# A graph layer whose edge attributes are copied by ScalarE into unused PSUM columns

## The reference

```python
h = jnp.maximum(_layernorm(x, axis=-1), 0.0)          # node_input
w = relu(radial @ W_fc1 / sqrt(10)) * sqrt(2) @ W_fc2 / sqrt(100)   # per edge, 192 wide
w0, w1, w2, w3 = (w[:, :64], w[:, 64:128], w[:, 128:160], w[:, 160:192])
y0 = l0[edge_src]; y1 = l1[edge_src]                  # rows of the linear map of h
e0 = edge_attr[:, :1]; e1 = edge_attr[:, 1:4]
m0 = w0 * y0 * e0
m1 = (w1 * y0)[:, :, None] * e1[:, None, :]
m2 = (w2 * e0)[:, :, None] * y1
m3 = w3 * jnp.einsum('eud,ed->eu', y1, e1) * INV_SQRT3
s0 ... s3 = segment_sum(m0 ... m3, edge_dst)
o0 = (s0 @ W_l2_00 + s3 @ W_l2_10) * a / FAN_L2
o1 = (s1 @ W_l2_01 + s2 @ W_l2_11) * a / FAN_L2
return x + concat(si0 + 0.5 * o0, si1 + 0.5 * o1)
```

## Time and profile before

| | |
|---|---|
| median of 3 runs | 2946.77 us |
| lowest, highest | 2910.21, 2948.76 us |
| the profiled execution | 2931.67 us |
| its span, first to last instruction | 2929.9 us |
| mean granted TensorE clock | 0.749 of full |
| busy: TensorE, VectorE, GpSimd, ScalarE | 2518.0, 1661.1, 1617.6, 340.0 us |
| GpSimd's idle time before its gathers | 1274.2 us |

### The profile page before, as it was taken

One profiled execution on the slowest core, in us unless ns is written; L12 is line 12 of the kernel. 1 busy time (PEld: TensorE's weight loads), 2 busy tenths in 40 slices (PEclk: granted clock), 3 DMA queues, 4 the chain that ended last, 5 costly groups with the idle time before them and its releaser, 6 DMA issues.

```text
span 2929.9 us, 41982 instructions
## 1 busy us (share of the span) xinstructions
PE 2518.0 (86%) x11466; PEld 2003.8 (68%) x11466; DVE 1661.1 (57%) x4639; ACT 340.0 (12%) x636; POOL 1617.6 (55%) x1637
## 2 busy tenths in 40 slices
PE   6889888788989988888888888898888889898888
PEld 6667776667767766666666666676676677676677
DVE  5455656556656556555655555565565556556555
ACT  5000111011101011010101101010110111011111
POOL 4645555555655555545555554555465555555553
PEclk8566778787767687877777777777778777677876
DMA  4212222222222222212222221222122222222221
GB/s 132 58 45 52 54 55 54 51 53 53 56 50 55 53 52 56 52 47 55 50 53 50 54 55 48 52 51 56 46 60 51 50 52 54 50 55 52 51 53 36
DMA packets 160622, 158.30 MB, mean 54 GB/s; under 512 B 87570, under 2 KB 132534, under 8 KB 160602
## 3 DMA queue, kind: packets, MB, share of 16 engines
q0 software_dynamic: 77376, 132.16, 18.3%
q1 hardware_dynamic: 82088, 24.49, 3.7%
q10 hardware_dynamic: 1138, 1.43, 0.1%
HBM read 149.90 MB, written 8.03 MB: 54 GB/s over the span
## 4 chain that ended last, share of the span: by engine, by line
PE 57%; another core or an unknown queue 15%; DVE 13%; issue 10%; DVEq 4%; ACT 1%; DMA 0%; POOL 0%; ACTq 0%; SPq 0%; POOLq 0%
PE ps_w L894 16%; PE ps_s L922 14%; PE ps_s L924 12%; PE ps_h L887 11%; DVE hot L686 3%; DVEq L745 2%; DVE acc L742 2%; DVE dot L661 2%; DVE dots L656 2%; DVE msg L677 1%; DVE hot L680 1%; PE ps_s L910 1%; DVEq L742 1%; PE ps_s L906 1%
## 5 line engine op out<-in xcount | busy, mean ns | idle before, releaser
L381 POOL DMA_INDIRECT y<-table,idx x1612 | 1583.6, 982 | 1274.2 <-DVE msg L677 657.4
L894 PEld LDWEIGHTS ps_w<-w_fc,hr 100*128 100x128 f32 x3224 | 682.8, 241 | 456.9 <-issue 404.2
L894 PE MATMUL ps_w<-w_fc,hr 100*128 100x192 f32 x3224 | 839.2, 417 | 49.2 <-issue 26.8
L922 PE MATMUL ps_s<-hot,msg 128*128 128x128 f32 x3216 | 612.8, 346 | 136.5 <-DVE msg L677 84.9
L922 PEld LDWEIGHTS ps_s<-hot,msg 128*128 128x128 f32 x3216 | 569.3, 255 | 180.6 <-DVE msg L677 111.8
L742 DVE TENSOR_TENSOR acc<-acc,ps_s 64x32 f32 (+1 forms) x1612 | 327.1, 203 | 628.8 <-remote 346.7
L887 PE MATMUL ps_h<-rad,w_fc 10*100 10x512 f32 x806 | 556.8, 775 | 80.0 <-ACT hid_t L492 43.4
L924 PE MATMUL ps_s<-hot,msg 128*128 128x64 f32 x3216 | 531.6, 314 | 88.1 <-issue 87.7
L924 PEld LDWEIGHTS ps_s<-hot,msg 128*128 128x128 f32 x3216 | 521.0, 241 | 94.6 <-issue 94.2
L487 ACT ACTIVATE hr<-ps_h 100x512 f32<-100x512 f32 x403 | 239.3, 597 | 2409.4 <-remote 1012.6
L667 DVE TENSOR_TENSOR msg<-ps_w,y 128x512 f32<-128x512 f32 x404 | 278.9, 690 | 340.9 <-remote 163.9
(11 more groups left out here) (83 smaller groups left out, 537.4 us busy)
## 6 DMA issues: line engine op xcount, KB each, us to landing
y<-table,idx POOLq DMA_INDIRECT x1612
rad<-in_radial SPq DMA_DIRECT2D x202, 40.0 KB
xres<-in_x SPq DMA_DIRECT2D x7, 560.0 KB, 4.7
out<-xres SPq DMA_DIRECT2D x49, 80.0 KB
table<-y SPq DMA_DIRECT2D x6, 560.0 KB, 3.2
idx<-in_src SPq DMA_DIRECT2D x202, 4.0 KB
attr_sb<-in_attr SPq DMA_DIRECT2D x202, 16.0 KB
dst_i<-in_dst ACTq DMA_DIRECT2D x1, 808.0 KB, 7.2
```

What stands on the lines that cost most here:

```text
L381: nc.gpsimd.indirect_dma_start(out=y[:, j, t, :], out_offset=None, in_=table, in_offset=bass.IndirectOffsetOnAxis(ap=idx[:, j // HALF, col ...
L894: ins = nc.tensor.matmul(ps_w[:, s, t, 0:NW], hr[:, s, t * P:(t + 1) * P], w_fc2[:, :], start=True, stop=True)
L922: nc.tensor.matmul(ps_s[:, s, 0:4 * W], msg[:, s, t, 0:P], hot[:, s, t, 1:V, :], start=(t == 0), stop=(t == T - 1))
```

## The change

ScalarE gets an operation more for each group, `move_attr`, right behind the relu. It copies the group's 16 attributes of each partition from `attr_sb` into columns 192 to 195 of the four tiles of `ps_w[:, s]`. It waits for the load of the attributes (which VectorE waited for before) and for the messages of group g - 2, which had that buffer. `edge_dots` and `weigh` read the attributes there. So that the copy, fc2's writes and VectorE's reads of a buffer of `ps_w` never run at the same time, `fc2` waits for the copy (`attr_moved`), and VectorE waits for the copy and for `fc2_done` ahead of `edge_dots`, and not ahead of `scalar_products` as before. In the last group `weigh` also stands behind the wait for fc2.

```diff
@@ functions of the attributes @@
+        def attr_behind(s, a, b, lo=0, hi=T):
+            return ps_w[:, s, lo:hi, NW + a:NW + b]
...
@@ ScalarE @@
+            def move_attr(i, j, first):
+
+                g, s = i * G + j, j % 2
+                if j % HALF == 0:
+                    act.wait_ge(ld_attr[j // HALF], i * 16 + 16)
+                if first:
+                    act.wait_ge(l_done, CHUNKS * NU)
+                else:
+                    act.wait_ge(msg_done, (g - 1) * 4)
+                nc.scalar.activation(attr_behind(s, 0, 4), attr_of(j, 0, 4), ACT.Copy).then_inc(attr_moved, 1)
...
                 def pair(k, first, finish):
                     for j in range(2 * G):
                         relu(k * (2 * G) + j, j % 2, first and j < 2)
+                        move_attr(k * 2 + j // G, j % G, first and j < 2)
...
@@ VectorE @@
-            def edge_dots(j, lo=0, hi=T):
+            def edge_dots(j, factors, lo=0, hi=T):
 
                 nc.vector.tensor_tensor(dots[:, lo:hi, :, :], vectors(j, lo, hi),
-                                        attr_of(j, 1, 4, lo, hi).unsqueeze(3).to_broadcast([P, hi - lo, 3, MUL1]),
+                                        factors.unsqueeze(3).to_broadcast([P, hi - lo, 3, MUL1]),
                                         ALU.mult).then_inc(dots_done, 1)
...
-            def weigh(g, j, s):
+            def weigh(g, s):
                 dve.wait_ge(hot_done, g + 1)
                 nc.vector.tensor_tensor(hot[:, s, :, 1:V, :], hot[:, s, :, 0:1, :].to_broadcast([P, T, 4, W]),
-                                        attr_of(j, 0, 4).unsqueeze(3).to_broadcast([P, T, 4, W]), ALU.mult).then_inc(msg_done, 1)
+                                        attr_behind(s, 0, 4).unsqueeze(3).to_broadcast([P, T, 4, W]), ALU.mult).then_inc(msg_done, 1)
 
             def messages(i, j):
                 g, s = i * G + j, j % 2
-                if j % HALF == 0:
-                    dve.wait_ge(ld_attr[j // HALF], i * 16 + 16)
                 which(g, s)
                 dve.wait_ge(gathered[j], i * (16 * T) + 16 * T)
-                edge_dots(j)
-                weigh(g, j, s)
+                dve.wait_ge(attr_moved, g + 1)
+                dve.wait_ge(fc2_done, g + 1)
+                edge_dots(j, attr_behind(s, 1, 4))
+                weigh(g, s)
                 dve.wait_ge(dots_done, g + 1)
                 sum_dots()
-                dve.wait_ge(fc2_done, g + 1)
                 scalar_products(j, s)
                 vector_products(j, s)
                 dve.wait_ge(dot_done, g + 1)
@@ TensorE @@
             def fc2(g, s):
 
                 pe.wait_ge(relu_done, g + 1)
+                pe.wait_ge(attr_moved, g + 1)
```

More of the change, by code:

```diff
@@ L181, in gnn_layer @@
         hot_done = sem("hot_done")
+        attr_moved = sem("attr_moved")
         dots_done = sem("dots_done")
@@ L208, in last_products, with attr_of @@
             return ps_h[:, b - IN_LOOP, 2 * P:2 * P + C]
+        def attr_of(j, a, b, lo=0, hi=T):
+            return attr_sb[:, j // HALF, (j % HALF) * T + lo:(j % HALF) * T + hi, a:b]
+        def attr_behind(s, a, b, lo=0, hi=T):
+            return ps_w[:, s, lo:hi, NW + a:NW + b]
         def by_path(eng, windowed, general):
@@ L516, in windowed @@
                     relu((TURNS - 1) * G + j, j % 2, False)
+                    move_attr(TURNS - 1, j, False)
                 for n, b in enumerate(range(IN_LOOP, BLOCKS)):
@@ L649, in _ @@
             dve.wait_ge(zeroed, 1)
-            def attr_of(j, a, b, lo=0, hi=T):
-                return attr_sb[:, j // HALF, (j % HALF) * T + lo:(j % HALF) * T + hi, a:b]
-            def edge_dots(j, lo=0, hi=T):
+            def edge_dots(j, factors, lo=0, hi=T):
                 nc.vector.tensor_tensor(dots[:, lo:hi, :, :], vectors(j, lo, hi),
-                                        attr_of(j, 1, 4, lo, hi).unsqueeze(3).to_broadcast([P, hi - lo, 3, MUL1]),
+                                        factors.unsqueeze(3).to_broadcast([P, hi - lo, 3, MUL1]),
                                         ALU.mult).then_inc(dots_done, 1)
@@ L707, in last_messages @@
                 g, j, s = EDGE_GROUPS - 1, LEFT - 1, (EDGE_GROUPS - 1) % 2
-                if j % HALF == 0:
-                    dve.wait_ge(ld_attr[j // HALF], TURNS * 16)
                 which(g, s)
-                weigh(g, j, s)
+                dve.wait_ge(attr_moved, g + 1)
                 dve.wait_ge(fc2_done, g + 1)
+                weigh(g, s)
                 for h in range(2):
@@ L715, in last_messages @@
                     dve.wait_ge(last_rows[h], 16 * (T // 2))
-                    edge_dots(j, lo, hi)
+                    edge_dots(j, attr_behind(s, 1, 4, lo, hi), lo, hi)
                     scalar_products(j, s, lo, hi)
@@ L781, in general @@
                     dve.wait_ge(g_rows, g * (16 * T) + 16 * T)
-                    edge_dots(0)
+                    edge_dots(0, attr_of(0, 1, 4))
                     dve.drain()
```

## The result

The changed kernel takes 2996.78 us (median of 6, 2983.57 to 3025.64), the kernel before 2947.77 us (6 runs, 2910.21 to 2956.69): a ratio of 1.021, 95% interval 1.013 to 1.028. It is slower, by about the 2% that can be told. The forecast was 2981 in a range of 2830 to 3120. Its terms, however, were mostly of the wrong size, and made up for each other. Where a kernel's own runs spread by more than 1.5%, its slowest runs are left out of ratio and interval, so a ratio can differ from the quotient of the medians given with it.

The account below looks back on a forecast made before the run. TensorE was taken as the bound, with the edge stage a cycle of gather bursts and rests. Sum: 2931.7 + 2 - 40 + 100 - 26 + 13 = 2981 us; range 2830 to 3120, likeliest case 2920 to 3005.

Parts of the forecast that it names:

- Operand reads: VectorE's dots (L656) and weighing (L686) from PSUM: +5 ns each, 403 times; 0 to 4 us, taken as +2.
- Gathers beside VectorE: GpSimd gathers no longer lengthened beside dots and weighing: 48 us may go; 0 to -60, taken as -40 us.
- The new wait: VectorE waits for fc2 before the dots, so messages come up to 1.69 us later: 0 to 260, taken as +100 us.
- Bursts that break: Later messages split GpSimd's gather bursts of three groups into faster bursts of two: 0 to -144, taken as -26 us.
- ScalarE's copy: 0.3 us per copy, showing where TensorE waits for the relu before fc2 (L894), 45 times: taken as +13 us.

Follow-up runs that it names:

- paired run with SBUF operands: Changed kernel with its copy, waits and order, but dots and weighing read attributes from SBUF, second chip: 2972.53 us, 1.010 of before; changed kernel there 3025.77 us, 1.028.
- the copy alone: Changed kernel with ScalarE's copy and fc2's wait for it, but VectorE reads SBUF and waits at the old place, first chip: 2873.47 us, 1.011 of before.
- the 1.042 run: Changed kernel, but dots and their sum read SBUF ahead of the wait; only weighing reads PSUM behind it, first chip: 2943.82 us, 1.042 of before.
- the wait alone: Kernel before with VectorE's wait for fc2 moved ahead of the dots, no copy, attributes from SBUF, first chip: 2846.21 us, 1.003 of before.

## Why the prediction was right, and where it was not

The total was 16 us short (2997 for 2981), the sign was the forecast one, and the range held. The terms added up to +49 us, and the two medians lie 49 us apart; that they agree so well is luck. By the steps:

- **Operand reads, +2 us: right.** 554 and 680 ns for 551 and 685. The row of L667 was the right neighbour. The fixed parts that the Trainium skill gives (VectorE: DVE Perf Modes, the section on the SBUF errata) would have put 52 us on VectorE, an estimate; the traces show +3 and -5 ns an operation in its place.
- **Gathers beside VectorE, -40 us: right in size on GpSimd, wrong in sign for the kernel.** The excess beside L656 and L686 was all of the 59 us and not four fifths, gathers became 55 us shorter, and the longest fell from 1471 to 1175 ns, as the reading of the earlier trace rows had it. The Trainium skill, SBUF — State Buffer, Who interferes with whom, has it so for a second SBUF input, and the trace agrees: 4 lengthened gathers for 260. This is the step that failed: "It is in the bursts, hence on the cycle when the burst's end releases the rest". The paired run with SBUF operands shows that reading PSUM costs 53 us in place of saving 40, though VectorE's operations are no longer. The rests took the saved time and more (+92 us). On the third chip, where GpSimd never rests, the step was right: 65 us.
- **The new wait, +100 us: far too large.** Alone it gives 1.003, at most some 24 us on the first chip. On the second, copy and wait together with SBUF operands give 1.010, no more than the copy alone on the first (1.011). I had priced a wait by the work that it uncovers, in 38% of the rests, and took the rest's length to be that of VectorE's chain. The wait before the dots took over much of the waiting that the accumulation did before, 573 us down to 233.
- **Bursts that break, -26 us: the mechanism happened, the gain did not.** Rests went from 155 to 182, more than the 17 I had counted, and from 2.6 groups a burst to 2.2. I had read 7.39 against 6.36 us a group from one stretch of each kind. Counted over all bursts of the trace of before, from start to start, it is 7.18 us with three groups (63 bursts), 6.66 with two (60) and 9.67 with one (12): half of the gain that I took, and a loss where a single group is split off. In the changed kernel bursts of two are the rule (106), but at 6.97 us a group. Two stretches were too few to give a pace.
- **ScalarE's copy, +13 us: too small.** It lasts 181 ns in place of 300, and the copy alone costs 14 to 51 us. The waits before fc2 are 45 as before, and this count, like that of the waits for the message product, adds matmuls (14) and weight loads (31), so it stood for some 31 groups. What of the 1.1% lies in the chain relu, copy, fc2, what in the copy's own wait for the messages, and what in the block's steps behind it stays open.

With the measured terms: copy and wait with SBUF operands +1.0%, PSUM reads +1.8%, together 1.028 on the second chip, where the first comparison gave 1.021. Of what was to be seen in the profile after, the moved waits (228 places), the two durations, the mean gather below 960 ns and the greater number of rests came; longer rests did not (4.5 us, and above 4.7 was asked for if the wait counts), and the copy was shorter than said. TensorE's idle time for the message product grew by 130 us, where some 100 were forecast. The 118 waits that the forecast had read as places were weight loads (65) and matmuls (53) together, so that TensorE stood for a message in some 65 groups of 403.

What was shown: gathers are what makes the signals from TensorE late on the second chip (with a quarter of them: 0.646), a pause behind each gather helps there (0.934), and reading PSUM, which shortens the gathers, hurts there (1.028 for 1.010). That the last comes from the denser gathers fits these three, and the 954 ns of the 1.042 run; it is argued and not shown. Against it as the whole story stands that the wait alone, too, has shorter gathers than the copy alone on the same chip (973 and 987 ns) and costs little or nothing. The test that was to decide it, both kernels with the same pause, ran on a chip where the signals are on time. How the kernels compare there without the memset was not run. An estimate from the rows: 1612 gathers of 0.95 us with pauses of 0.30, and the 57 us outside them, are 2072 us of the 2117 that the kernel before takes there, so the change could win at most some 45 us.

## What to carry to other kernels

A faster engine off the chain gives nothing by itself: make the account of its whole span (work, pauses, rests by releaser) before and after, and see which item takes what another gives up. When the releasers are unnamed and come only as another engine stops, measure first what holds them, here by leaving out three of four gathers and by spacing them, before pricing any reordering. Run every version and the kernel before on one chip, and trace both there. And run the pair that differs only in the operand: a total near the forecast had hidden three terms of the wrong size and one of the wrong sign. When a view gives waits of TensorE, ask for matmuls and weight loads apart before counting places.

## What the runs showed of the hardware

- On two chips completion signals of TensorE reached the other engines late while GpSimd gave out indirect gathers of 0.95 us at pauses of 0.30 us (for example 104 unnamed releases of the relu with the wait alone, 728.8 us, and 108 in the changed kernel, 821.9 us). Matmul ends are modelled, and TensorE's matmuls also came singly there, so late signals and late work are not told apart. On a third chip all 403 relus were released by name, in each of the four kernels traced, all with a memset behind each gather; the one that on the second chip had 148 unnamed releases is among them. The kernel before takes 2824.51, 2944.76 and 2116.98 us on the three. What sets the chips apart stays open.
- So the best version depends on the chip: a 315 ns memset behind each gather gives 0.934 on the second and 1.173 on the third.
- A gather beside VectorE's two-SBUF-input operations took up to 1471 ns; with one of the inputs in PSUM the longest was 1175 ns, and the 260 lengthened gathers fell to 4.
- Behind a longer memset the mean gather was longer, 956, 994 and 1047 ns with 60, 240 and 440 columns, with a median of 952 ns in all three; the excess lies in the gathers that ran beside VectorE's dots or weighing. Why more of them were lengthened, and for longer, is not shown.
- The same 11466 TensorE instructions were busy for 1999.9 us at a granted clock of 0.953, 2264.7 at 0.831 and 2543.6 at 0.748, in the kernels with 60, 240 and 440 columns of memset on the third chip.
- ScalarE copied 128x16 fp32 values from SBUF to PSUM in 181 ns.
